# Six weight loads of the identity, without a product, ahead of the first edge product of each batch

## The chip, the core and the metric

The kernel runs on one core of one Trainium2 chip. The metric is the device time of one execution in microseconds (us), as the median of several runs. The engines of the core work in parallel and wait for each other through semaphores: TensorE (PE in the profile, with its weight loads listed apart as PEld), VectorE (DVE), ScalarE (ACT), GpSimd (POOL), and SyncE (SP), which issues transfers.

## The reference

One layer of a graph network on 12500 nodes of 256 features with 200000 edges, sorted by their target node. Of the normalized input xn it computes three things and adds them up:

```python
# graph attention, 4 heads of 64
h_src = (xn @ W_src).reshape(n, HEADS, OUT_DIM)
e = a_src[src] + a_dst[dst]
e = jnp.where(e > 0, e, NEG_SLOPE * e)
p = jnp.exp(e - m[dst])                      # m: maximum over the edges of a target
alpha = p / jnp.maximum(denom[dst], 1e-16)
out = segment_sum(alpha[:, :, None] * h_src[src], dst)
# linear attention ("mix"): Q K V products, merge, norm, two dense layers of 512
# afterwards, on the sum: 8 experts with three 256x256 products each, weighted by a router
```

The change touches the stage in which the first two of these run together.

## The kernel before, in words

The kernel has three stages. The first (up to about 310 us) projects the node features and writes a table of source features to HBM. The third (from about 3192 us) runs the experts, a stream of products on TensorE. Between them stands the merged loop, where the edges and the linear attention share the engines.

**The merged loop.** The edges are cut into tiles of 128. A step is 2 tiles (`DU`), a batch is 2 steps (4 tiles, `GU`), a group is 8 batches (`GQ`), and there are 55 groups, so 440 batches. For a batch GpSimd gathers 4 tiles of source rows of 260 values with four indirect transfers (L1107). VectorE multiplies them by the attention weights (`messages`, L1231), TensorE sums them by target with a one-hot matrix as weights (`aggregate`, L1655: two f32 products for each of the two steps), and VectorE adds the result to the running sum (`add`, L1245). The transfer of the sums to HBM goes out at the end of each batch.

At the same time TensorE prepares the next group q: `transpose` (L1630) turns the bf16 one-hot tiles of a batch with the identity as the moving operand, ScalarE copies the four results (`transposed`, L1451), and `dst_logits` (L1641) multiplies them as weights by 12 columns of the target logits. Single small transposes of the attention maxima (L1663 to L1702) stand between, one or two in each batch.

A chunk of the linear attention (512 nodes) is spread over the 16 batches of two groups: `mix_mid` (L1794) and `mix_end` (L1814) put one product step into each batch, for instance `hidden` (L1780, eight records of 512 columns), `output` (L1791), `merge` (L1758), each followed by a copy on ScalarE (L1524, L1496, L1505) for which the next step waits.

**Order.** Nothing is planned: each engine has its own instruction stream, written out by hand, and carries it out in that order. TensorE's is `turn` (L1822), called once for each group by `turns` (L377) through `ring` (L37), which makes a hardware loop over pairs of groups. In each batch b of a group the stream holds: the edge product of step 0 (`aggregate(g, s, b, 0)`), the transposes for the next batch of the next group, the edge product of step 1, the step of the linear attention, a small transpose, and the 12-column products of `look`. The first edge product of a batch waits for the messages (`msg_set`), for the one-hot copy (`s_ev`) and for a free bank of its three (`acc_add`). The last turn before the loop (`g is None`) has no edge products.

`identb` is the 128x128 identity in bf16, set once in the first stage; in the loop the transposes read it as their moving operand.

Of the kernel before, what the change touches and what calls it, by code (L numbers as in the profile page):

```python
# [71 lines left out]
def build(nc, a, out, N, E):  # L72
# [15 lines left out]
    with es:  # L88
# [191 lines left out]
        identb = r4.take(P // 2, dt=bf16)  # L280
# [83 lines left out]
        def step_values(engine, table, b, most):  # L364
            lo = b * BS
            sl = table[:, lo:lo + FETCH * BS] if isinstance(b, int) else table[:, bass.ds(lo, FETCH * BS)]
            return nc.values_load_multi_w_load_instructions(sl, engines=[engine], min_val=0, max_val=most,
                                                            skip_runtime_bounds_check_because=BOUND)[1]
# [667 lines left out]
        with nc.Block() as block:  # L1036
# [582 lines left out]
            def _(pe):  # L1619
                pe.wait_ge(ad_cut, 5)  # L1620

                def transpose(q, sq, b):
                    s_set.wait(pe, q, b + 1)
                    if b:
                        st_ev.wait(pe, q, b)
                    else:
                        st_ev.wait(pe, q - 1)
                        ad_sum.wait(pe, q - 1)
                    for u in range(GU):
                        ins = nc.tensor.transpose(T4[:, u * P:(u + 1) * P], SB[sq][b][:, u * P:(u + 1) * P], identb)  # L1630
                    ins.then_inc(t_mm.sem, 1)

                def dst_logits(q, b, js):

                    st_ev.wait(pe, q, b + 1)
                    if b == LB:
                        as_ev.wait(pe, q)
                    for u in range(GU):
                        v, k = (ps[4], D + (b * GU + u) * 3 * HEADS) if b < LB else (
                            ps[6], P + 2 * GS + ((b - LB) * GU + u) * 3 * HEADS)  # L1640
                        ins = nc.tensor.matmul(v[:, k:k + 3 * HEADS], ST[:, u * P:(u + 1) * P],  # L1641
                                               adf[:, bass.ds(js[u // DU], 1)].rearrange("p o h -> p (o h)"), start=True, stop=True)
                    ins.then_inc(d_mm.sem, 1)

                def aggregate(g, s, b, i):
                    k = b * BS + i
                    if i == 0:
                        msg_set.wait(pe, g, b + 1)
                        s_ev.wait(pe, g, b + 1)
                    if k >= BANKS:  # L1650
                        acc_add.wait(pe, g, k - BANKS + 1)
                    else:
                        acc_add.wait(pe, g - 1, 1 + max(j for j in range(NS) if j % BANKS == k))
                    for u in range(DU):
                        ins = nc.tensor.matmul(ps[k % BANKS][:, 0:MW], S32[b % 2][:, i * DU + u], G[s][:, b * GU + i * DU + u],  # L1655
                                               start=u == 0, stop=u == DU - 1)
                    ins.then_inc(g_mm.sem, 1)

                def spread(q):

                    dst_f.wait(pe, q)
                    z_set.wait(pe, q - 1, 2)
                    nc.tensor.transpose(ps[6][:, 0:P], dst4.rearrange("p h t -> p (h t)"), ident[:, :]  # L1663
                                        ).then_inc(db_tr.sem, 1)

                def end_dsts(q):

                    db_ev.wait(pe, q)
                    rs_exp.wait(pe, q - 1)
                    nc.tensor.transpose(ps[7][0:1, 0:P], dB[:, 0:1], ident[:, :])  # L1670
                    nc.tensor.transpose(ps[7][0:1, P:2 * P], dB[:, P - 1:P], ident[:, :]).then_inc(dc_tr.sem, 1)

                def logits(q):
                    as_cp.wait(pe, q)
                    db_ev.wait(pe, q)
                    nc.tensor.transpose(ps[6][:, 0:P], as_c.rearrange("p h t -> p (h t)"), ident[:, :]).then_inc(as_tr.sem, 1)

                def ends(q):
                    fb_set.wait(pe, q)
                    row_set.wait(pe, q, 2)  # L1680
                    dl_set.wait(pe, q)
                    nc.tensor.transpose(ps[7][0:1, 0:P], fw[:, P - 1:P], ident[:, :])
                    nc.tensor.transpose(ps[7][0:1, P:2 * P], bw[:, 0:1], ident[:, :]).then_inc(ft_tr.sem, 1)

                def carries(q):
                    uv_set.wait(pe, q)
                    pass_on(pe, "pe")
                    one = ident[0:1, 0:1]
                    nc.tensor.transpose(ps[7][:, 2 * P:2 * P + 1], uu.rearrange("p h t -> p (h t)"), one)
                    nc.tensor.transpose(ps[7][:, 2 * P + 1:2 * P + 2], vv.rearrange("p h t -> p (h t)"), one).then_inc(c_tr.sem, 1)  # L1690
# [103 lines left out]
                def mix_mid(n, i):  # L1794

                    cur, prev = chunks(n)
                    if cur and i in (0, 1):
                        q_product(n, i)
                    if prev and i in (9, 10):
                        output(n - 1, i - 9, n, cur)  # L1800
                    if cur and i == 3:
                        denominators(n)
                    if cur and i in (4, 5):
                        numerators(n, i - 4)
                    if cur and i == 6:
                        attended(n, 0)
                    if cur and i in (7, 8):
                        merge(n, i - 7)
                    if cur and i == 11:
                        m_turned(n, 0)  # L1810
                    if cur and i >= 12:
                        hidden(n, i - 12)

                def mix_end(n, i):  # L1814

                    cur, prev = chunks(n)
                    if cur and i == 6:
                        attended(n, 1)
                    if cur and i == 11:
                        m_turned(n, 1)  # L1820

                def turn(g, s, n, q, sq, nq, r):  # L1822
                    here, ahead = g is not None, q is not None
                    tiles_of = {}

                    def fetch(k):
                        js = step_values(ET.PE, j_step, q * GQ + k, NR - 1)
                        for i in range(FETCH):
                            tiles_of[k + i] = js[i * BS:(i + 1) * BS]

                    def look(k):
                        dst_logits(q, k, tiles_of.pop(k))
                    for b in range(GQ):
                        if here:
                            aggregate(g, s, b, 0)
                        if ahead:
                            if b == 1:
                                look(1)
                            if b < GQ - 1:
                                transpose(q, sq, b + 1 if b else 0)  # L1840
                        if here:
                            aggregate(g, s, b, 1)
                            mix_mid(n, s * GQ + b)
                        if ahead:
                            if b in (0, 3):
                                fetch(b + 1 if b else 0)
                            if b == 0:
                                spread(q)
                            if b == 1:
                                end_dsts(q)  # L1850
                            if b == 3:
                                logits(q)
                            if b == 4:
                                ends(q)
                            if b == 5:
                                carries(q)
                            if b == 6:
                                maxima(q, r)
                            if b == GQ - 1:
                                shrink(q)  # L1860
                            if b < GQ - 1:
                                look(b + 1 if b else 0)
                            if b == 0:
                                transpose(q, sq, 1)
                            if b == 5 and r is not None:
                                records(pe, r, q, REC_PS)
                        if here:
                            mix_end(n, s * GQ + b)
                            if isinstance(g, int) and (g, b) == (H0 + 4, 4):
                                xf_transpose(pe, 0)  # L1870
# [343 lines left out]
```

## Time and profile before

| | us |
|---|---|
| median of 3 runs | 4956.36 (4953.54 to 4975.74) |
| the profiled execution, its own time | 4960.95 |
| its span, first to last instruction | 4959.1 |
| merged loop | about 415 to 3192 |
| experts | 3192 to 4959 |
| granted TensorE clock, mean of the span | 0.926 |

The profile is one execution. Busy times are those of an engine's instructions; the idle time of an engine before an instruction is put down to what ended it, and "remote" there means that the releasing update could be matched to no instruction, "issue" that no wait explains it. The granted clock is 1.00 at 2.4 GHz and 0.50 at 1.2 GHz; a mean over a stretch lies between. TensorE shows two records (a load and a product, twice) for each f32 product.

### The profile page before, as it was taken

The numbers are of one execution on the slowest core, as the hardware profiler recorded it, in microseconds if no ns is written. First come the engines' busy times: TensorE is split into PE (matmuls) and PEld (weight loads), VectorE is DVE, ScalarE is ACT, GpSimd is POOL, SyncE is SP. The second block draws the span as 40 slices with busy tenths as digits, with TensorE's granted clock in tenths as the row PEclk, the third lists the DMA queues.
The fourth block names the chain that finished last, engine by engine and source line by source line (L and its number), as shares of the span: only waits on it lengthen the run. The fifth ranks groups of instructions, "written<-read, shape, count | busy, mean of one in ns | idle before, by whom it ended". The sixth has DMA issues, their size and how long they took to land. (4 is left out here: it accounts for less than half of the span.)

```text
span 4959.1 us, 82912 instructions
## 1 busy us (share of the span) xinstructions
PE 4271.0 (86%) x23402; PEld 3406.8 (69%) x23403; DVE 3603.9 (73%) x9152; ACT 2332.6 (47%) x4488; POOL 1765.9 (36%) x1802
## 2 busy tenths in 40 slices
PE   8955878888787888778888886799999999999999
PEld 7844555565565555555555654588888888888888
DVE  8845666676666766666666767788778878877886
ACT  5632333333333333333333332366666666666666
POOL 2245565565565656555665655200000000000000
PEclk9977998899989989899988887899999999999999
DMA  6544555555555555555555555400000000000000
GB/s 202 188 129 111 139 156 142 141 142 142 148 151 143 143 142 153 144 141 140 147 152 145 144 137 160 121 22 27 26 16 23 26 26 13 26 26 26 14 25 18
DMA packets 344855, 510.25 MB, mean 103 GB/s; under 512 B 43529, under 2 KB 268417, under 8 KB 344705
## 3 DMA queue, kind: packets, MB, share of 16 engines
q0 software_dynamic: 84480, 234.40, 19.6%
q1 hardware_dynamic: 260224, 274.20, 17.1%
q8 instruction: 50, 0.82, 0.1%
q14 instruction: 101, 0.82, 0.1%
HBM read 325.55 MB, written 182.89 MB: 103 GB/s over the span
## 5 line engine op out<-in xcount | busy, mean ns | idle before, releaser
L1107 POOL DMA_INDIRECT acc<-h_tab,strips x1760 | 1690.8, 961 | 1158.7 <-issue 500.6
L1655 PE MATMUL ps<-acc 128*128 128x260 f32 x3520 | 1107.7, 446 | 55.0 <-issue 24.3
L2077 PE MATMUL ps<-part,part 128*128 128x256 f32 (+1 forms) x3168 | 1073.4, 339 | 15.3 <-ACT part L2031 9.3
L2079 PE MATMUL ps<-part,part 128*128 128x256 f32 (+1 forms) x3168 | 1064.4, 336 | 0.0
L2078 PE MATMUL ps<-part,part 128*128 128x256 f32 (+1 forms) x3168 | 1063.7, 336 | 0.0
L1245 DVE SCALAR_TENSOR_TENSOR acc<-acc,strips,ps 128x260 f32<-128x260 f32 x880 | 421.7, 479 | 512.7 <-remote 287.7
L1655 PEld LDWEIGHTS ps<-acc 128*128 128x128 f32 x3520 | 689.4, 216 | 149.4 <-issue 50.6
L2077 PEld LDWEIGHTS ps<-part,part 128*128 128x128 f32 x3168 | 596.5, 188 | 83.3 <-ACT part L2031 9.7
L1451 ACT ACTIVATE strips<-ps 128x512 bf16<-128x512 bf16 x440 | 262.3, 596 | 816.8 <-remote 539.6
L2079 PEld LDWEIGHTS ps<-part,part 128*128 128x128 f32 x3168 | 596.3, 188 | 69.5
L2078 PEld LDWEIGHTS ps<-part,part 128*128 128x128 f32 x3168 | 596.8, 188 | 66.3
L1231 DVE TENSOR_TENSOR acc<-acc,ps 128x1024 f32<-128x1024 f32 x440 | 533.0, 1211 | 10.2 <-ACT acc L1482 4.9
L2029 ACT ACTIVATE strips<-ps,bn 128x512 f32<-128x512 f32 (+1 forms) x400 | 310.6, 776 | 454.7 <-PE ps L2079 449.1
L1780 PE MATMUL ps<-acc,keep 128*128 128x512 f32 x800 | 373.0, 610 | 38.9 <-ACT work L1524 23.7
L1961 DVE TENSOR_TENSOR part<-strips,part 128x512 fp32r<-128x512 f32 (+1 forms) x400 | 259.9, 679 | 144.4 <-ACT part L2031 132.6
L1967 DVE TENSOR_TENSOR part<-acc,part 128x512 fp32r<-128x512 f32 (+1 forms) x400 | 261.0, 677 | 129.5 <-ACT part L2045 129.5
L2043 ACT ACTIVATE acc<-ps,bn 128x512 f32<-128x512 f32 (+1 forms) x400 | 309.9, 775 | 66.5 <-PE ps L2079 66.5
L2031 ACT ACTIVATE part<-ps,bn 128x512 fp32r<-128x512 f32 (+1 forms) x400 | 307.9, 770 | 0.0
L2045 ACT ACTIVATE part<-ps,bn 128x512 fp32r<-128x512 f32 (+1 forms) x400 | 306.0, 765 | 0.0
L1641 PE MATMUL ps<-strips 128*128 x1760 | 126.8, 173 | 198.8 <-ACT strips L1451 138.5
L1641 PEld LDWEIGHTS ps<-strips 128*128 128x128 bf16 x1760 | 108.8, 101 | 274.7 <-issue 258.3
L1780 PEld LDWEIGHTS ps<-acc,keep 128*128 128x128 f32 x800 | 154.9, 196 | 201.7 <-issue 164.9
(267 smaller groups left out, 6348.6 us busy)
## 6 DMA issues: line engine op xcount, KB each, us to landing
side_tab<-acc SPq DMA_DIRECT2D x440, 260.0 KB
acc<-h_tab,strips POOLq DMA_INDIRECT x1760
acc<-xnt_tab SPq DMA_DIRECT2D x50, 512.0 KB
h_tab<-proj SPq DMA_DIRECT2D x25, 520.0 KB, 7.0
proj<-in_x SPq DMA_DIRECT2D x25, 512.0 KB, 5.4
base_tab<-proj SPq DMA_DIRECT2D x25, 512.0 KB, 3.2
xnt_tab<-proj SPq DMA_DIRECT2D x25, 512.0 KB, 6.1
work<-base_tab SPq DMA_DIRECT2D x25, 512.0 KB
```

Of the source, the lines that this page charges most:

```text
L1107: pool.indirect_dma_start(G[s][:, b * GU + u], None, h_tab, bass.IndirectOffsetOnAxis(REC[s][:, b * GU + u, 0:1], 0)).then_inc(g_in[s], 16)
L1231: nc.vector.tensor_tensor(m, m, f.unsqueeze(3).broadcast_to([P, GU, HEADS, HB - 1]), ALU.mult).then_inc(msg_set.sem, 1)
L1245: nc.vector.scalar_tensor_tensor(A[:, k % (RB * BS)], A[:, (k - 1) % (RB * BS) if k else RB * BS], smt[s][:, k:k + 1], ps[k % BANKS][:, 0: ...
L1655: ins = nc.tensor.matmul(ps[k % BANKS][:, 0:MW], S32[b % 2][:, i * DU + u], G[s][:, b * GU + i * DU + u], start=u == 0, stop=u == DU - 1)
L1780: ins = nc.tensor.matmul(MIX[:, :], w1[:, k, m * P:(m + 1) * P], rhs, start=k == 0, stop=k == 3)
L2029: nc.scalar.activation(AR[:, m, cut(c)], ps[m][:, cut(c)], ACT.Relu, scale=bn[:, i:i + 1], bias=bn[:, 16 + i:17 + i])
L2031: nc.scalar.activation(AHI[e % 2][:, m, cut(c)], ps[m][:, cut(c)], ACT.Relu, scale=bn[:, i:i + 1], bias=bn[:, 16 + i:17 + i]).then_inc(a_e ...
L2043: nc.scalar.activation(BR[:, m, cut(c)], ps[2 + m][:, cut(c)], ACT.Relu, scale=bn[:, 32 + i:33 + i], bias=bn[:, 48 + i:49 + i])
L2045: nc.scalar.activation(BHI[e % 2][:, m, cut(c)], ps[2 + m][:, cut(c)], ACT.Relu, scale=bn[:, 32 + i:33 + i], bias=bn[:, 48 + i:49 + i]).th ...
L2077: nc.tensor.matmul(o, x[0], y[0], start=first, stop=False)
L2078: nc.tensor.matmul(o, x[0], y[1], start=False, stop=False)
L2079: return nc.tensor.matmul(o, x[1], y[0], start=False, stop=last)
```

## The change

A new function in TensorE's block loads the bf16 identity as weights six times, and `turn` calls it ahead of the first edge product of each batch that has one. The loads carry no wait and no semaphore update, and no product uses them: the next instruction is the weight load of the edge product itself.

```diff
+                def keep_busy():
+
+                    for _ in range(6):
+                        nc.tensor.ldweights(identb)
+
                 def aggregate(g, s, b, i):
...
                     for b in range(GQ):
                         if here:
+                            keep_busy()
                             aggregate(g, s, b, 0)
                         if ahead:
                             if b == 1:
```

## Rows read from the trace of the kernel before

**Rows 1.** The page: span, busy times, and of the 40 slices PE and its clock.

```profile
span 4959.1 us, 82912 instructions
...
PE 4271.0 (86%) x23402; PEld 3406.8 (69%) x23403; DVE 3603.9 (73%) x9152; ACT 2332.6 (47%) x4488; POOL 1765.9 (36%) x1802
...
PE   8955878888787888778888886799999999999999
...
PEclk9977998899989989899988887899999999999999
```

**Rows 2.** Busy time of each engine by stretch: merged loop, then experts.

```profile
core 0: us, PE busy (x) PEld busy (x) DVE busy (x) ACT busy (x) POOL busy (x), PEclk, DMA share, GB/s
...
415.00:3192.00 2777.00, 2220.39 (x11175) 1604.26 (x11173) 1900.19 (x4799) 968.28 (x2176) 1636.29 (x1700) 0.89 0.53 144
3192.00:4959.00 1767.00, 1745.14 (x10296) 1532.74 (x10296) 1415.35 (x3434) 1176.16 (x1752) 0.89 (x1) 1.00 0.08 24
```

**Rows 3.** Who waited for whom in the merged loop: total, times, longest (us).

```profile
ACT strips L1451 <- remote: 508.7, 136, 9.7
...
POOL acc L1107 <- PE ps L1655: 325.9, 164, 19.7
DVE acc L1245 <- remote: 287.7, 131, 6.5
...
DVE acc L1245 <- PE ps L1655: 202.0, 201, 3.7
ACT strips L1451 <- PE ps L1630: 187.2, 148, 10.7
...
PE ps L1641 <- ACT strips L1451: 136.9, 65, 6.5
```

**Rows 4.** One standstill and its surroundings, stretch by stretch, columns as in rows 2.

```profile
1515.50:1524.60 9.10, 8.87 (x47) 5.73 (x47) 7.28 (x25) 2.57 (x5) 6.70 (x7) 1.00 0.53 146
1524.60:1527.90 3.30, 0.02 (x1) 0.00 (x0) 0.37 (x3) 0.59 (x2) 0.95 (x1) 0.99 0.31 82
1527.90:1531.26 3.36, 3.30 (x4) 1.52 (x5) 3.23 (x9) 1.30 (x4) 2.30 (x3) 0.50 0.17 42
1531.30:1545.00 13.70, 13.70 (x56) 7.87 (x54) 8.43 (x23) 5.78 (x15) 7.20 (x8) 1.00 0.42 111
```

**Rows 5.** Products of the merged loop, grouped by line: busy, mean ns, idle before.

```profile
L1655 PE MATMUL ps<-acc 128*128 128x260 f32 x3513 | 1104.2, 446 | 54.4 <-issue 24.3 <-DVE acc L1245 22.4 <-DVE acc L1231 2.5
...
L1641 PE MATMUL ps<-strips 128*128 x1728 | 124.0, 173 | 177.7 <-ACT strips L1451 136.9 <-issue 40.2
...
L1676 PE MATMUL ps<-ident,strips 128*128 128x128 f32 x54 | 20.1, 373 | 101.6 <-ACT strips L1466 91.2 <-issue 6.6 <-ACT strips L1451 3.6
```

**Rows 6.** The line of the 12-column products: duration min/median/max in ns.

```profile
L1641 PEld LDWEIGHTS ps<-strips x1728: 95/98/184, 416.7 to 3166.4; 128*128 128x128 bf16 x192
L1641 PE MATMUL ps<-strips x1728: 167/168/219, 416.8 to 3166.4; 128*128 x192
```

**Rows 7.** The timeline of TensorE: start, length (us), line; first at 2.4 GHz.

```profile
1504.50 0.25 PE L1641 MATMUL ps<-strips 128*128 x4
1504.61 1.12 PE L1655 MATMUL ps<-acc 128*128 128x260 f32 x4
...
1510.18 0.25 PE L1641 MATMUL ps<-strips 128*128 x4
1510.28 1.12 PE L1655 MATMUL ps<-acc 128*128 128x260 f32 x4
```

**Rows 8.** The timeline of TensorE in a stretch at 1.2 GHz.

```profile
1808.29 0.35 PE L1641 MATMUL ps<-strips 128*128 x4 [3.44 <-issue]
```

## Prediction

> **What bounds the kernel now.** I read the page first. TensorE is busy for 86% of the span, but its digits fall from 9 to about 8 between the first and the last quarter, and its clock digits fall with them [rows 1]. So I cut the span by stage. In the experts TensorE is busy for 1745 of 1767 us at clock 1.00, and the change has nothing there. In the merged loop, 2777 us long, it is busy for 2220, at a mean clock of 0.89; VectorE has 1900 and GpSimd 1636 [rows 2]. TensorE is idle there for 2777 - 2220 = 557 us. With two clock levels a mean of 0.89 means that (1 - 0.89) / 0.5 = 22% of the loop, 611 us, ran at 1.2 GHz.
>
> Next the waits of the loop. Gathers wait 326 us for edge products, VectorE's adds 202 us, ScalarE's copies 187 us for transposes, and TensorE in turn 137 us for those copies [rows 3]. That is a ring: TensorE produces, a copy or add answers, TensorE goes on, and there is no other work in its stream meanwhile. The biggest rows have no known releaser: 509 us at the copies, 288 us at the adds [rows 3]. I looked at one such place closely. From 1524.6 to 1527.9 us TensorE does 0.02 us of work, VectorE 0.37, ScalarE 0.59, GpSimd 0.95; then all start together, and the next 3.4 us run at clock 0.50 before it is 1.00 again [rows 4]. So standstills of the whole core exist that no engine's length explains, and the clock falls behind them. I can't tell from this trace what ends them.
>
> The loop is therefore bound by TensorE plus round trips, with standstills between. An instruction added to TensorE's stream lengthens it unless it falls into an idle stretch.
>
> **What the change adds.** 440 batches with 6 loads each are 2640 loads, so the count of PEld should go from 23403 to about 26043. Nothing is removed or moved, no wait or transfer is added, and SyncE's, GpSimd's, VectorE's and ScalarE's streams stay as they are. Two terms decide: what the loads cost, and what they do to the clock.
>
> *Cost of a load alone.* The trace has no load without a product, so I bound it. The nearest rows are those of the 12-column products, whose loads have the same shape and type (128x128 bf16) and whose products are so short that the load sets the pace. Four such products take 0.25 us together [rows 7] and one lasts 0.168 [rows 6], so the step from one load-and-product pair to the next is (0.25 - 0.168) / 3 = 0.027 us at 2.4 GHz. At 1.2 GHz it is (0.35 - 0.168) / 3 = 0.061 [rows 6, 8]. Six loads cost 0.16 or 0.36 us, mixed by the shares of the clock 0.78 x 0.16 + 0.22 x 0.36 = 0.20 us per batch, and 440 x 0.20 = 90 us of TensorE time in all. The upper bound is that a load without a product can't overlap the next: then it costs its own median duration, 0.098 us [rows 6], six cost 0.59, and the loop gets 440 x 0.59 = 259 us. The lower bound is zero: the loads have no wait, and could all run beside products in flight. I take the 27 and 61 ns, since that row differs from the new instruction by one tiny product only.
>
> The Trainium skill, "TensorE: Matmul & The Clock Gate", section "LDWEIGHTS (loading the stationary operand)", gives columns divided by 1.2 GHz, which is an estimate of 107 ns for 128 columns and 2640 x 0.107 = 282 us; the trace speaks against it as a step between loads, since pairs follow each other at 27 ns, and its section on weight-path perf modes names a faster path for full non-fp32 weights that fits better.
>
> *What hides it.* TensorE's idle time just ahead of edge products is 54 us in all [rows 5], so few of the loads can be free by standing in a wait. The instruction ahead is in many batches a short one: the 12-column products start 0.11 us before the edge product [rows 7], which is no cover either. So nearly all of the 90 us extends TensorE's own stream. How much of that reaches the end depends on the later idle stretches. Those that end on an answer to TensorE's own work stay as long as they are, and move. Those that end at a time of their own shrink: the copies and adds that wait for an unknown releaser, 509 and 288 us [rows 3], are of a size with the 557 us of idle time. I take half as absorbed, so 90 / 2 = 45 us reach the end. The bounds of this term are 0 and 90.
>
> *What the clock gives back.* The whole pot: TensorE is busy for 80% of the time (2220 of 2777), so of the 611 us at 1.2 GHz about 490 are work, and at 2.4 GHz that work would take about half, a gain of at most 245 us. To reach it the loads would have to stand in the idle stretches. They don't: the waits stand ahead of the 12-column products (178 us) and of the transpose of the source logits (102 us), in the middle and at the end of a batch; ahead of the edge products there are 54 [rows 5]. Where TensorE waits for something, the loads have run already. They still make it busy a little longer in each batch, 0.20 us of 2777 / 440 = 6.3. I give them 15 us, 6% of the pot, between bounds of 0 and 245.
>
> **Sum.** 45 - 15 = +30 us. The profiled execution took 4960.95 us, which makes 4991; the median of the runs stands 4.6 lower, so the prediction is 4986 us, +0.6%. A measurement of this kernel can tell about 0.5%, 25 us, from no change.
>
> **The rivals.**
>
> *Nothing reaches the end.* The loads overlap products in flight, or all the added time is taken up by stretches that end at times of their own, or a small clock gain cancels it. The time is then 4956 within 20 us. For it: the 796 us of unknown releases. Against it: the adds and gathers also wait over 500 us for edge products directly. The skill page named above says in its section on what happens when a matmul is issued that TensorE pulls weight loads ahead of products in flight; by that rule the load of the first identity could hide, but those behind it have no product to hide beside. That the loads do not do what they are for (no product, so no activity for the clock) belongs here too. Chance 0.20.
>
> *The loads are serial.* Each takes its full 0.098 us, one behind the other, as it would if a load had to end before the next one starts. Then 259 us are added to the stream, and by half to all of them reach the end: 4956 + 130 to 259 = 5086 to 5215. For it: in every row of the trace each load is followed by its product, so overlap between two bare loads is not shown. Against it: the 27 ns step. The skill's 107 ns would give 5097 to 5238. Chance 0.12.
>
> *The clock stays up (faster).* If the chip counts a weight load as activity, each batch starts with a block of it, and in stretches where TensorE was busy for only part of the time the clock might not fall, or rise sooner after the standstill. Its place is the batch after an idle stretch, as at 1527.9 us [rows 4]. It decides from the point where more than 45 of the 245 us are recovered, 18%. At half the pot the time is 4956 + 45 - 122 = 4879; at a third, 4919. For it: the clock is down for 22% of the loop. Against it: the loads stand where TensorE is rarely idle, and the idle stretches last microseconds against 0.16. Chance 0.20.
>
> **How the numbers follow.** The forecast has 0.48 and reaches from +5 to +90 us, 4961 to 5046. Its part under 4981 counts as no change (0.10), the rest as slower (0.38). With the serial loads slower has 0.50; with "nothing" no change has 0.30; faster has 0.20. The range leaves out most of the serial case and the far part of the clock case: 4910 to 5110 us. The forecast's own range is 4961 to 5046.
>
> **What would show it.** PEld has 2640 records more, and bf16 loads of the identity follow each other at about 27 ns at clock 1.00. The step from the 12-column products to the edge product grows from 0.11 to about 0.27 us. The mean clock of the loop stays near 0.89; at 0.92 or more the clock case is right, and if it stays and the time falls, my reading of the standstills is wrong. TensorE's idle time in the loop falls by about 45 us. If the new loads are 98 ns apart, the serial case holds. What would upset all of it: the standstills. If adding instructions shifts them, a few per cent of their sum either way is as large as the forecast. The experts must keep their 1767 us.

## The result, and the profile after

The changed kernel took 5037.63 us in the median of 4 runs (5021.02 to 5059.22) against 4955.33 for the kernel before on the same chip: 82 us more, a ratio of 1.016 with a 95% interval of 1.0135 to 1.0185. The direction was right and the size was not: +82 against the forecast of +30. The time lies inside the range and even inside the forecast's own 4961 to 5046, but by luck, as nearly half of the growth stands where the prediction had put nothing. The profiled execution took 5059.22 us, the slowest of the four, so its rows show 98 us where the medians show 82.

The page of the changed kernel: span, busy times, TensorE's clock in 40 slices, and the DMA queue that brings instructions (packets, MB, share).

```profile
span 5057.4 us, 85575 instructions
...
PE 4353.2 (86%) x23402; PEld 3526.5 (70%) x26043; DVE 3602.7 (71%) x9152; ACT 2335.9 (46%) x4488; POOL 1763.5 (35%) x1802
...
PEclk9977998898889898889988997899999999999999
...
q8 instruction: 142, 2.33, 0.2%
```

PEld has 26043 records in place of 23403 [rows 1], the 2640 loads. That queue moved 142 packets. The page of the kernel before has this line for it:

```profile
q8 instruction: 50, 0.82, 0.1%
```

Now the stretches of the changed kernel, cut at the first and the last edge product: merged loop, then experts. Columns: stretch, length, busy time (count) of PE, PEld, DVE, ACT, POOL, clock, DMA share, GB/s.

```profile
412.50:3252.40 2839.90, 2298.13 (x11186) 1724.65 (x13820) 1900.26 (x4819) 970.83 (x2178) 1635.01 (x1700) 0.89 0.50 141
3252.40:5057.40 1805.00, 1753.57 (x10296) 1534.78 (x10296) 1416.41 (x3434) 1177.44 (x1752) 0.57 (x1) 0.99 0.08 25
```

Cut in the same way, the loop of the kernel before lasts 2781 us, from 410.7 to 3192.0, and its experts 1767 [rows 2]. So 59 us came in the merged loop, where the loads are, and 38 in the experts' stage, of which the change alters no instruction. The two stretches are nearly two separate questions. (For the medians' 82 us, 38 in the experts leave 44 for the loop.)

**In the loop.** The busy time of TensorE's products grew from about 2225 to 2298 us, so its idle time fell by 15 us (2781.3 - 2224.7 = 556.6, 2839.9 - 2298.1 = 541.8), where the prediction's list of signs had 45; the clock stayed at 0.89 [rows 2]. The loads, by their own line (duration min/median/max in ns):

```profile
L1648 PEld LDWEIGHTS <-strips x2640: 95/96/152, 411.7 to 3250.3; 128*128 128x128 bf16 x189
```

and on the timeline at full clock, six of them ahead of an edge product:

```profile
1512.02 0.29 PEld L1648 LDWEIGHTS <-strips 128*128 128x128 bf16 x6
1512.26 0.74 PEld L1660 LDWEIGHTS ps<-acc 128*128 128x128 f32 x4
```

Six take 0.29 us and one lasts 0.096, so the step is (0.29 - 0.096) / 5 = 0.039 us: more than the 0.027 of a load with its tiny product, and far less than one load after the other. The edge product's own load starts 0.24 us behind the first of them, so the loads take up to 440 x 0.24 = 106 us of TensorE time at full clock. The stream grew by a little less. Where an edge product follows right behind the four 12-column products, the median step from the first of those to the edge product is 104 ns at full clock in the kernel before (183 places) and 322 here (184 places): 0.22 us more, or 96 us over 440 batches. In this execution 59 us reached the end of the loop.

**In the experts.** The waits of TensorE between 3500 and 5000 us (total, times, longest):

```profile
PEld ps L2083 <- issue: 36.4, 20, 2.1
PE ps L2083 <- issue: 29.9, 20, 1.9
```

and one of the places, on the timeline of the weight loads:

```profile
3557.11 0.19 PEld L2085 LDWEIGHTS ps<-part,part 128*128 128x128 f32 x1
3559.15 0.19 PEld L2083 LDWEIGHTS ps<-part,part 128*128 128x128 f32 x1 [1.85 <-issue]
3559.26 0.19 PEld L2084 LDWEIGHTS ps<-part,part 128*128 128x128 f32 x1
3559.49 0.19 PEld L2085 LDWEIGHTS ps<-part,part 128*128 128x128 f32 x1
3559.72 0.19 PEld L2083 LDWEIGHTS ps<-part,part 128*128 128x128 f32 x1
3559.95 0.19 PEld L2084 LDWEIGHTS ps<-part,part 128*128 128x128 f32 x1
3560.19 0.19 PEld L2085 LDWEIGHTS ps<-part,part 128*128 128x128 f32 x1
3562.17 0.19 PEld L2083 LDWEIGHTS ps<-part,part 128*128 128x128 f32 x1 [1.79 <-issue]
```

TensorE stands twice in quick succession, waits for no semaphore either time ("issue"), and this comes ten times, some 145 us apart: the experts' hardware loop has 11 rounds, so 10 branches back. The loads' idle time at these twenty stops, 36.4 us, is nearly the whole 38. Between the two stops of a pair there are always six loads, and 826 from there to the next pair. The kernel before has no such wait at this line (its L2077) between 3440 and 4900 us. These waits, and 92 more packets of instructions, are what the experiments had to explain.

### The profile page after: what moved, and what is told of

Read it like the earlier page. It is cut to its first block and busy times, and to the rows that moved or that the text cites. A ratio compares the mean times of both kernels' runs of the same rounds, so it can differ in the third digit from the quotient of the medians.

```text
span 5057.4 us, 85575 instructions
## 1 busy us (share of the span) xinstructions
PE 4353.2 (86%) x23402; PEld 3526.5 (70%) x26043; DVE 3602.7 (71%) x9152; ACT 2335.9 (46%) x4488; POOL 1763.5 (35%) x1802
## 3 DMA queue, kind: packets, MB, share of 16 engines
q8 instruction: 142, 2.33, 0.2%
## 5 line engine op out<-in xcount | busy, mean ns | idle before, releaser
L1660 PE MATMUL ps<-acc 128*128 128x260 f32 x3520 | 1133.9, 454 | 88.3 <-DVE acc L1245 35.3
```

## The experiments

The chip that a set of kernels runs on is not the same from one set to the next, and the kernel before took 4955, 4359, 5009, 5012 and 5009 us on them. I therefore compare with the kernel before of the same set. The experts' stage is nearly the same on all chips; the merged loop is not. The stretches and clocks below are from one profile of each kernel, the ratios from all its runs.

### First set: is it the place of the code?

**16 and 528 instructions ahead of everything.** Identity loads run once, where TensorE waits anyway, none in the batches:

```diff
+                for _ in range(16):          # second kernel: 528
+                    nc.tensor.ldweights(identb)
                 pe.wait_ge(ad_cut, 5)
```

> The kernel before, with 16 identity loads run once on TensorE at the start of the merged stage, where TensorE idles for some 100 us anyway; no loads in the batches. The change made the experts' stage 38 us longer (1767 to 1805 us) although no instruction of it changed, and its instruction queue moved 142 packets in place of 50. Theory A (code position): the 528 loads that the change adds to TensorE's program in front of the experts' loop push that loop to a place where it is fetched again in every round; 528 instructions are 2 packets of 16 KB and 16 instructions over, if one takes 64 bytes as the Trainium skill says of a matmul (TensorE: Matmul & The Clock Gate, 'What happens when you issue a matmul'). If only the place within a packet matters, these 16 loads alone give about 140 packets and +30 to +38 us. Theory B (the experts' extra time belongs to that one execution, or to something the batches leave behind): 50 packets and 4955 within 15 us.

> The kernel before, with 528 identity loads run once on TensorE at the start of the merged stage, as many instructions as the change adds to the program, none in the batches; they take some 21 us at 40 ns each, inside an idle stretch of about 100 us. Theory A (code position): the experts' stage grows from 1767 to about 1805 us, the instruction queue moves about 140 packets, and the time is +35 to +45 us with the merged loop unchanged at about 2780 us. Theory B (loads in the batches cause all of it): no change, 4955 within 15 us, 52 or so packets.

Ratios 1.0000 (0.9990 to 1.0009) and 1.0003 (0.9993 to 1.0012). The queue's lines, first of the kernel with 16, then with 528:

```profile
q8 instruction: 50, 0.82, 0.1%
```

```profile
q8 instruction: 52, 0.85, 0.1%
```

Their experts' stages lasted 1766.4 and 1766.7 us. So neither the growth of the program by 528 instructions nor the place of the experts' loop counted from the start of the program does it.

**The change with 240 more loads there.**

```diff
+                for _ in range(240):
+                    nc.tensor.ldweights(identb)
                 pe.wait_ge(ad_cut, 5)
```

> The changed kernel, with 240 more identity loads run once at the start of the merged stage, so that TensorE's program grows by 768 instructions in all, which is three packets of 16 KB. Theory A (code position, place within a packet): the experts' stage is back at 1767 us with about 53 packets, and what is left is the cost of the loads in the loop, +45 to +60 us over the kernel before. Theory B: as the changed kernel, +82 us. A third reading, that any growth of the code ahead makes the loop refetch: the experts stay at about 1805 us and the total at +82.

It took 4397 against 4359 us, ratio 1.0087 (1.0070 to 1.0104). Its stretches, merged loop and experts, behind them those of the kernel with 16 loads:

```profile
370.70:2594.40 2223.70, 2046.68 (x11186) 1574.90 (x13820) 1885.65 (x4820) 977.87 (x2178) 1654.82 (x1722) 0.98 0.65 181
2594.40:4398.80 1804.40, 1753.39 (x10296) 1534.78 (x10296) 1417.07 (x3434) 1176.94 (x1752) 0.45 (x1) 0.99 0.08 25
```

```profile
370.90:2593.80 2222.90, 2025.18 (x11186) 1486.51 (x11186) 1888.47 (x4819) 980.45 (x2178) 1661.97 (x1722) 0.97 0.65 181
2593.80:4360.20 1766.40, 1746.52 (x10297) 1534.08 (x10296) 1414.93 (x3434) 1176.27 (x1752) 0.58 (x1) 1.00 0.08 24
```

On this chip six loads per batch cost the merged loop 1 us in the profiles, and all of the 38 us stood in the experts. My forecast for this kernel, experts back at 1767, was wrong: counting from the start of the program gives nothing.

**Twelve loads.**

```diff
-                    for _ in range(6):
+                    for _ in range(12):
```

> The changed kernel with twelve loads in each batch in place of six. In the trace of the changed kernel the loads follow each other at 40 ns at full clock, 0.24 us for six, 106 us over 440 batches, of which 59 us reached the end of the merged loop. Theory 1 (loads cost TensorE time and about half is absorbed): the merged loop is 2781 + 2 x 59 = about 2900 us. Theory 2 (the loads keep the clock up or fill waits once there are enough of them): less than 2 x 59 and a mean clock in the loop above 0.90. Theory 3 (no slack is left after six): 2840 + 106 = about 2950 us. The experts' stage tells of the code position on its own: this program grows by 1056 instructions.

4443 us, ratio 1.0196 (1.0179 to 1.0213). The merged loop lasted 2284.7 us, 62 more than with none, at clock 0.97, and the experts 1787.6: 21 more, not 38. The cost in the loop is therefore not proportional to the number of loads: on this chip nothing for the first six and 62 us for the second six.

### Second set: the place of the code, counted from where?

**The change itself, once more.**

> The changed kernel itself, once more, because the chip of the last four runs took 4359 us for the kernel before where the first took 4956: its merged loop lasted 2223 us and not 2781, with 155 us at the lower clock and not 626. On that chip six loads with 240 padding loads left the merged loop at 2224 us and took 38 us more in the experts' stage. If the loads are free in a loop without standstills, the changed kernel has its merged loop within 10 us of the kernel before, the experts' stage at about 1805 us and the total at +35 to +40 us. If the chip is again one with standstills (about 4956 us), the total is +82 us.

5066.6 against 5009.1 us, ratio 1.0114 (1.0089 to 1.0138), experts 1805.4 us. A chip like the first. With 38 us in the experts, 57.5 - 38, about 19, are left for the loop; the same subtraction on the first chip gives 82 - 38 = 44.

**Loads only in the hardware loop; and 336 loads behind it, none in the batches.**

```diff
                         if here:
-                            keep_busy()
+                            if not isinstance(g, int):
+                                keep_busy()
```

```diff
                 turns(pe, turn, True)
+                for _ in range(336):
+                    nc.tensor.ldweights(identb)
```

The second is an edit of the kernel before.

> The six loads only in the batches of TensorE's hardware loop (46 of the 55 groups), not in the two groups ahead of it and the seven behind it, so the loop's body is as long as in the changed kernel but the code between it and the experts' loop is as before. The code-position theory in its first form has fallen: 16 and 528 instructions ahead of everything left 50 to 52 instruction packets and the experts at 1767 us. Two forms are left. Theory P (position after the loop: the 336 instructions in the seven groups behind it count): 50 packets, experts 1767 us, total within 10 us of before. Theory L (length of the merged loop's body, 465 program instructions before and 562 with the change): 142 packets, experts about 1805 us, total +35 to +40.

> The kernel before, with 336 identity loads run once at the end of the merged stage's TensorE program, as many as the change puts into the seven groups behind the loop; no loads in the batches. They cost at most 336 x 0.040 = 13 us. Theory P (position after the loop): 142 packets, experts' stage longer by some 38 us beside the 13, total +40 to +50. Theory L (length of the loop's body): 50 to 52 packets, total 0 to +13.

Ratios 1.0054 (1.0027 to 1.0080) and 1.0071 (1.0046 to 1.0097). The queue's lines, loop only first:

```profile
q8 instruction: 140, 2.29, 0.2%
```

```profile
q8 instruction: 141, 2.31, 0.2%
```

Each of my two theories had one of these at 50. Both fell as they stood, and together they suggested the rule: a longer body of the merged loop and more code behind it act alike, code ahead of it does not act. What counts is the distance from the head of the merged loop to the head of the experts' loop. The kernel's text has the reason: `ring` (L37) gives the merged loop's head a fixed slot in its block of instructions (`head_slot`, 0), whatever stands ahead of it. I counted TensorE's instructions in the compiled programs. Against the kernel before, the distance grew by 0 in the two kernels of the first set without loads in the batches, by 433 in the change (97 in the loop's body, one of them a register copy, and 336 behind it) and in the kernel with 240 more ahead, by 865 with twelve loads, by 97 with the loads in the loop only, by 336 here, and by 864 with the products below, each of which is a load and a product. An instruction has 64 bytes in the compiled program, and the packets have 16 KB. The Trainium skill, "Runtime: NRT & Kernel Launch", section "Instruction fetch mechanics", says that instructions come in blocks of 16 KB, 256 instructions each; the queue's packets agree in size (2.33 MB / 142). By remainders of 256:

| distance, remainder | kernels | packets | experts, us |
|---|---|---|---|
| 0 | 16 ahead; 528 ahead | 50; 52 | 1766.4; 1766.7 |
| 80 | 336 behind | 141 | 1796.1, with up to 13 of the loads |
| 97, products 96 | loop only; twelve; products (below) | 140; 143; 143 | 1787.3; 1787.6; 1787.3 |
| 177 | change; again; 240 ahead | 142; 142; 143 | 1805.0; 1805.4; 1804.4 |

Three different kernels on two chips with remainders of 96 and 97 agree to 0.3 us. With 80, 96 and 97 there is one stop at each of the ten branches back, with 177 two. A stop of the kernel with the loads in the loop only:

```profile
3549.39 0.19 PEld L2086 LDWEIGHTS ps<-part,part 128*128 128x128 f32 x1
3551.39 0.19 PEld L2084 LDWEIGHTS ps<-part,part 128*128 128x128 f32 x1 [1.81 <-issue]
```

**Products in place of loads.**

```diff
+                    if i == 0:
+                        for _ in range(6):
+                            nc.tensor.matmul(ps[k % BANKS][:, 0:P], identb, identb, start=True, stop=True)
                     for u in range(DU):
```

> The changed kernel with six real products in place of the six bare loads (identity times identity, 128 columns, into the bank that the edge product then overwrites, behind the same waits as the edge product). At full clock a transposing product of this shape follows the one before at 55 ns, so six take 0.33 us where six bare loads take 0.24. If only products keep the clock up, the time at 1.2 GHz in the merged loop falls clearly below that of the bare loads (109 us with loads, 155 without, on the chip of the last runs) and the merged loop is no longer than with loads. If the clock sees both alike, the loop is longer by up to 440 x 0.09 = 40 us than with the bare loads.

5070 us, ratio 1.0112 (1.0077 to 1.0146). Its merged loop:

```profile
411.70:3293.60 2881.90, 2365.07 (x13823) 1748.92 (x13820) 1902.39 (x4818) 970.19 (x2177) 1635.04 (x1700) 0.90 0.50 139
```

and that of the change in the same set:

```profile
410.90:3268.20 2857.30, 2287.80 (x11186) 1724.94 (x13820) 1897.74 (x4819) 971.06 (x2178) 1641.05 (x1700) 0.88 0.50 140
```

The clock is a little higher with products, 0.90 against 0.88, and the loop 25 us longer. At the lower clock the loop spent 584 us with products, and 624 to 704 in the thirteen other profiles on chips of about 5000 us. So products seem to keep the clock up better than bare loads, on the word of one profile, and they did not pay for themselves.

### Third set: the aligned change

The distance is set back to the kernel before plus a multiple of 256, by loads run once behind the merged loop: 79 with six loads, 159 with twelve, 128 with the loads ahead of the 12-column products. At 0.040 us each these extra loads take up to 3, 6 and 5 us themselves, which are in the times below.

```diff
                 turns(pe, turn, True)
+                for _ in range(79):
+                    nc.tensor.ldweights(identb)
```

The last kernel has this beside it:

```diff
                     def look(k):
+                        if here:
+                            keep_busy()
                         dst_logits(q, k, tiles_of.pop(k))
                     for b in range(GQ):
                         if here:
-                            keep_busy()
                             aggregate(g, s, b, 0)
```

> The kernel before itself, for a profile on the same chip as the three that follow. The kernel before took 4956, 4359 and 5009 us in three calls on different chips, and the difference lay in the merged loop; its experts' stage should be 1767 us again with 50 instruction packets, whatever the loop takes.

> The changed kernel with 79 more identity loads run once at the end of the merged stage, so that the distance from the head of the merged loop to the head of the experts' loop differs from the kernel before by 512 instructions, two packets of 256, and not by 433. So far 0 left the experts at 1767 us; 80 and 97 (a remainder by 256) gave 1783 to 1787, 177 gave 1805. Theory P (position, counted from the merged loop's head): 50 to 53 packets, experts 1767 us plus the 3 us of the 79 loads, total 36 us less than the changed kernel: on a fast chip the kernel before within 8 us, on one with standstills +20 to +45. Theory that any growth behind the loop makes it refetch: 142 packets and 1805 us again.

> Twelve loads per batch, with 159 more at the end of the merged stage, so that the distance between the loops' heads differs by 1024 instructions. Theory P: 50 to 54 packets and experts at 1767 plus 6 us. What is left is the cost of twelve loads in the merged loop alone: on a fast chip about +61 us, as with the unaligned twelve; on a chip with standstills, if half of 2 x 106 us is absorbed, +100.

> The same six loads, but ahead of the 12-column products in each batch and no longer ahead of the first edge product, with the experts' loop at the distance of the kernel before plus 512. TensorE's biggest idle time is in front of these products (178 us in the kernel before, 54 ahead of the edge products). Theory 1 (a load costs what TensorE has no idle time for): 10 to 40 us less in the merged loop than with the loads ahead of the edge product. Theory 2 (what is absorbed is absorbed anywhere in the ring): the same time within 10 us. Theory 3 (the clock profits from loads next to idle stretches): the time at 1.2 GHz in the loop falls below that of the kernel before by over 10% and the loop is shorter than before.

| kernel | us | ratio to before (interval) | merged loop | experts | packets |
|---|---|---|---|---|---|
| before, again | 5017.4 | 1.0009 (0.9992 to 1.0027) | 2833.9 | 1767.2 | 50 |
| six, aligned | 5027.2 | 1.0031 (1.0015 to 1.0047) | 2845.7 | 1767.7 | 52 |
| twelve, aligned | 5052.6 | 1.0076 (1.0055 to 1.0098) | 2874.6 | 1770.0 | 54 |
| at the 12-column products | 5062.0 | 1.0092 (1.0063 to 1.0121) | 2887.2 | 1768.5 | 52 |

The aligned kernels have their experts back, within 3 us and with the extra loads partly in that stretch. The merged loop of the kernel before on this chip, then the queue's line and both stretches with six loads:

```profile
410.80:3244.70 2833.90, 2250.92 (x11186) 1613.95 (x11186) 1899.24 (x4819) 966.25 (x2178) 1633.50 (x1700) 0.88 0.51 141
```

```profile
q8 instruction: 52, 0.85, 0.1%
```

```profile
411.20:3256.90 2845.70, 2297.18 (x11186) 1730.70 (x13831) 1898.39 (x4820) 969.50 (x2178) 1634.39 (x1700) 0.88 0.51 141
3256.90:5024.60 1767.70, 1746.40 (x10296) 1536.56 (x10366) 1415.00 (x3434) 1175.86 (x1752) 0.45 (x1) 0.99 0.08 24
```

By the medians the loads' own price is thus 15 us (0.31%) for six and 40 us for twelve, extra loads included. Put ahead of the 12-column products, six loads in 432 of the batches cost 50 us. All three of my theories for that place were wrong: TensorE has its biggest idle time there, and the loads cost three times as much. Idle ahead of those products was 232.8 us in this kernel, with the loads between:

```profile
L1641 PE MATMUL ps<-strips 128*128 x1728 | 123.9, 173 | 232.8 <-ACT strips L1451 189.4 <-issue 42.1 <-DVE acc L1245 0.2
```

The loads carry no wait, so they run before the wait of the products, and the idle time did not shrink: it is 177.7 us in the kernel before [rows 5], and 177 on the chip of this set too. The time at the lower clock did not fall either, 701 us in both. Why the same loads cost 50 us there and 15 ahead of the edge product, I have not tested.

### Fourth set: is it a wait for instructions?

The merged loop has a branch hint on TensorE, the experts' loop has none. In `ring` the hint also sets the slot of the loop's head. The edit, in the change and in the kernel before:

```diff
-                ring(pe, NCH, 2, body)
+                ring(pe, NCH, 2, body, hint=True)
```

> The changed kernel, side by side with the aligned one below on one chip. Experts' stage 1805 us with 142 packets, total 36 to 38 us over the aligned kernel.

> The changed kernel with the 79 loads that put the experts' loop back at its distance. Its difference to the kernel before is the cost of six loads in the merged loop alone: +15 us on the chip of the last call, and by subtraction +44 on the first and 0 on the fast one. If the cost hangs on the chip's standstills it is near 0 on a chip at 4359 us and +15 to +44 on one at about 5000; its difference to the changed kernel is 36 to 38 us on any chip.

> The kernel before with the same hint. Its experts' loop has no idle stretch at the branch back (TensorE busy for 1745 of 1767 us, and the idle time stands at the stage's start), so nothing is to be won: within 5 us of the kernel before. It tells whether the hinted head alone changes the number of packets.

| kernel | us | ratio to before (interval) | experts | packets |
|---|---|---|---|---|
| change | 5059.3 | 1.0100 (1.0084 to 1.0115) | 1806.5 | 142 |
| change, aligned | 5027.7 | 1.0039 (1.0025 to 1.0052) | 1766.6 | 52 |
| change, hinted | 5028.0 | 1.0036 (1.0023 to 1.0049) | 1765.3 | 52 |
| before, hinted | 5007.8 | 1.0002 (0.9988 to 1.0015) | 1767.5 | 51 |

The experts' stretch of the changed kernel with the hint:

```profile
3245.00:5010.30 1765.30, 1745.20 (x10297) 1533.48 (x10296) 1415.09 (x3434) 1176.73 (x1752) 0.50 (x1) 1.00 0.08 24
```

No load or product was taken away, the code is one instruction longer, and the stops are gone together with 90 packets. Both remedies give the same time within 0.3 us, 31 to 32 us less than the change. Since the hint in this kernel both fixes the head's slot and announces the branch, its two halves are not told apart.

**A count of blocks.** The slots in the compiled programs fit all kernels. In them a round of the experts' loop has 1722 TensorE instructions: 816 products in the kernel's text, each a load and a product, 16 of them (the router's) two of each, so 832 loads, as the trace has them between stops, 832 products and 58 others. Count from the merged loop's head at slot 0 of a block of 256, labels left out, and the experts' head is at slot 66 in the kernel before, the kernels with 16 and 528 loads ahead and the aligned ones, at 146, 162 and 163 with remainders of 80, 96 and 97, at 243 in the change, and at 0 with the hint. From 66 or 0 the loop touches seven blocks, and no kernel with seven had these stops; from the others it touches eight, and every kernel with eight had them. At 243 the head's block holds only 13 instructions of the loop, six loads with their products and one other, and the second stop stands behind exactly six loads. So TensorE waits there for the next block, which is the reason for two stops in place of one.

## Why the prediction was right or wrong

**The step that failed** is the sentence on the experts, "the change has nothing there", and with it the check that they "must keep their 1767 us". They grew by 38 us, nearly half of the 82. I had asked of each term where it stands in TensorE's stream, and never what the added code does to the code behind it. The cause is the place of the experts' loop in its blocks of instructions, set by the distance between the heads of the two hardware loops: shown by 0, 80, 97 and 177 as remainders, by a kernel in which the program grew just as much without effect, and by two remedies that leave the loads in place. That the stop is a wait for instructions is shown by the packets (50 to 54 without stops, 140 to 143 with them), by the branches back, and by the second stop at the end of a block. Why eight blocks do not stay and seven do is only argued: the Trainium skill, in the section named above, gives TensorE room for 2048 instructions, which is eight blocks, so that with one fetched ahead seven would fit and eight would not. No run here took the fetching ahead apart.

**The cost of a load.** I had 27 ns at full clock and 61 at half, and measured 40 and 47 (medians of the steps). The first was too low, the second too high. At full clock the stream grew by 0.22 us per batch where I had 0.16, at half clock six loads take 6 x 0.047 = 0.28 where I had 0.36. Mixed as in the prediction, 0.78 x 0.22 + 0.22 x 0.28 = 0.23 us, an estimate of 103 us in all: my 90 came near it because two errors partly cancel. The upper bound of 98 ns one after the other, and the rival that rested on it, fell with the step of 40. The Trainium skill's 107 ns is not the step between loads either.

**What hides it.** Half, I said. What reached the end was 44 us by subtraction on the chip of the prediction, where the loop's forecast was 45 - 15 = 30, and less on the others: 15 and 19 us in the direct measurements with the experts' term removed, about 19 by subtraction in the second set, and nothing on the fast one. The forecast lies among these, which says that half is of the right size and no more. Why the first chip shows more is open; its merged loop was shorter than that of the third set's chip, 2781 us against 2834, and single profiles of kernels without a load in the batches differ by as much as 13 us (2833.9 and 2846.8).

**The clock.** I gave the loads 15 us of 245 and they earned none that can be seen on chips like the first: the time at the lower clock was 626 to 704 us in the four profiles without loads in the batches and 642 to 678 in the six with six loads ahead of each edge product. On the fast chip it fell, from 155 and 158 us without loads in the batches to 109 with six and 124 with twelve. An estimate from these: half of the 46 to 49 us, some 24, was won back with six. That may be a part of why they were free there; the rest of their 96 us must have fallen into waits. The faster rival needed 18% of the pot, and it did not come: the loads have run before TensorE begins to wait. The Trainium skill's page "TensorE: Matmul & The Clock Gate", section "What's actually happening", says that activity releases the throttle; the products of the second set agree with it weakly, 0.90 against 0.88.

**The standstills.** My reading that they belong to no engine's length got support I had not asked for. On the fast chip the merged loop is 2223 us long, and the list of its waits begins with these:

```profile
POOL acc L1107 <- issue: 502.9, 1651, 0.3
ACT work L1524 <- PE ps L1782: 318.7, 100, 4.6
ACT strips L1451 <- PE ps L1632: 309.6, 276, 13.6
```

This is the kernel with 16 loads ahead, which took as long as the kernel before. The waits for an unknown releaser, 509 and 288 us in the kernel before [rows 3], are absent from the list, while on the chip of the third set they are back for the kernel before:

```profile
ACT strips L1451 <- remote: 493.6, 134, 12.3
...
DVE acc L1245 <- remote: 316.3, 129, 7.2
```

So the standstills differ between chips (or with what else differed between the sets) and not between these kernels. What they are stays open.

## What to carry to other kernels

When code is added inside or behind a hardware loop, look at the loops that follow, too: the instruction queue's packet count and stops marked "issue" at a branch back tell of code that is fetched again. Here a branch hint on that loop, or code that moved its head to another slot, removed it. Work that is meant to keep TensorE's clock up must not run ahead of the wait that it is to fill: loads without a wait of their own did, even where TensorE waits most, and lengthened the stream (50 us). Whether it helps to hold them back until then, no run here shows. Weigh a change of one per cent against the kernel before on the same chip, since the chips here differed by 15% on the same program.

## What the runs showed of the hardware that I had not expected

- A loop of 1722 TensorE instructions branched back 10 times with 50 to 54 instruction packets in the whole kernel where it touches seven blocks of 256 (those over 50 go with longer programs), and with about 9 packets more for each branch back (140 to 143 in all) where it touches eight, which cost 1.6 to 3.8 us each time (16 to 38 us).
- Bare weight loads of 128x128 bf16 follow each other at 39 to 40 ns at full clock, slower than a load with a product of 12 columns (27 ns), and at 47 ns at half clock, faster than such a pair (61 ns).
- Six such loads per batch were free on a fast chip and six more cost 62 us.
- The same program took 4359 us on one chip and 4955 to 5012 on others. In the profiles (on the fast chip that of the kernel with 16 loads ahead) the difference to the first chip is 40 us before the merged loop, 558 in it and 1 in the experts' stage.
